# Who issues the six transfers that stack the second block's keys: SyncE's queue or ScalarE's

## The chip, the cores and the metric

The program runs on one core of a Trainium2 chip. The metric is the device time of one execution in microseconds (us). The core's engines run side by side, each through its own list of instructions, and wait for one another by semaphores: TensorE (PE in the profile; PEld is its weight load), VectorE (DVE), ScalarE (ACT), GpSimd (POOL) and SyncE (SP), which does nothing here but issue DMAs.

## The reference

32 images (12 x 224 x 224) are summed over patches of 16 x 16 and projected to 196 tokens of 192 channels; 77 text tokens are put behind them, so an image has T = 273 tokens. Two transformer blocks follow, each with 12 heads of 16 channels:

```
h = concat([tokens(x), txt])
h = h + quantised_attention_0(layernorm(h))
h = h + mixture_of_depth_block(layernorm(h))      # routed attention or mean mixing, then a GELU FFN
h = h + attention_1(layernorm(h))                 # softmax attention, what this change is about
h = h + experts(layernorm(h))                     # one shared and three routed SiLU experts, best two count
```

In `attention_1`, q and k are 12 x 273 x 16 each, and the scores q k^T are wanted nearly in float32 precision.

## The kernel before

The work on one image is cut into stages with short names. A turn, listed by hand in `TURN`, holds each stage once, for different images: a stage with offset 2 works on the image that a stage with offset 0 had two turns ago. Every engine goes through the stages of `TURN` in that order and does its own part of each, if it has one. There are 36 turns (32 images, and the turns in which the pipeline fills and drains); in steady state one turn finishes one image. TensorE's results go to four PSUM areas, A, B, M and N, with a pair of semaphores each: `full` (TensorE has written) and `taken` (it has been read, and the next stage may begin).

The change is at the start of a turn, in these stages:

- `n4f`: the normed tokens of the second block are transposed by TensorE and copied by ScalarE (L605).
- `qk1.0`, `qk1.1`: TensorE projects them to queries (area A) and keys (area B). ScalarE evicts each twice, as float32 (L654) and as bfloat16 (L658). VectorE makes two further bfloat16 pieces from the rest (L925 to L927), so that three pieces add up to nearly the float32 value. `parts_ready` counts 1 when the queries' pieces are there and 2 when the keys' are.
- The stack: a bfloat16 matmul over 96 rows gets the precise scores when the pieces are stacked, six blocks of 16 rows, in `q1s` and `k1s`. Each block is a transfer from `parts` (96 partitions) into 16 partitions of `q1s` or `k1s`; there are six for the queries and six for the keys, and all twelve count on `stack_in` (L457, issued by SyncE at `qk1.0` and `qk1.1`).
- `v2`: TensorE and VectorE.
- `n0f`: ScalarE copies the transposed tokens of another image (L599). `qk0.0`, `qk0.1`: TensorE and VectorE, then four small transfers each by SyncE (L450, `q0s` and `k0s`). `pool.0` between them: VectorE reduces a slice of an image, and SyncE issues the load of another one (L430).
- `n2f`: TensorE transposes, ScalarE copies with scale and bias (L584) and so frees area M. `ey.0`: TensorE (area A), `Silu` by ScalarE (L679). `v1`: TensorE, which needs the copy of `n2f` and area M (L1042), then VectorE (L828). `ez.0`: VectorE. `ey.1`: TensorE (area B).
- `mx.0`: the first of 36 matmuls (L1259) whose row maxima VectorE takes (L938). It waits for all twelve transfers of the stack. The other 35 are spread over the following third of the turn, between other stages.

`a0.0` (L1117), some way behind, is the first stage that waits for `q0s` and `k0s`. The queue of ScalarE holds only computation before the change.

Of the kernel before, what the change touches and what calls it, by code (L numbers as in the profile page):

```python
# [21 lines left out]
H, HD = 12, 16  # L22
# [18 lines left out]
Q_PARTS = (0, 0, 1, 0, 2, 1)  # L41
K_PARTS = (0, 1, 0, 2, 0, 1)
# [6 lines left out]


TURN = """
tok n4s n4n n4f cw n0s n1s n2n n0n qk1.0 qk1.1 v2 n0f qk0.0 pool.0 qk0.1 n2f ey.0 v1 ez.0 ey.1 mx.0 mx.1 mx.2 n1n gate
mx.3 ez.1 mx.4 pool.1 k1 mx.5 v0 a0.0 mx.6 mx.7 ey.2 cl.0 cl.1 ez.2 mx.8 r3 mx.9 mx.10 rta a0.1 cl.2 dy.0 cl.3 pk0
a0.2 mx.11 mx.12 mx.13 mx.14 mx.15 pk1 ey.3 ez.3 mx.16 r2 mx.17 gt mx.18 vs mx.19 pv.0 mx.20 og.0 mx.21 s1.0 mx.22
mx.23 s1.1 r1 mx.24 ey.4 ez.4 ey.5 mx.25 ez.5 t1.0 mx.26 mx.27 t1.1 mx.28 rtb mx.29 cl.4 mx.30 cl.5 a0.3 c1 mx.31
# [6 lines left out]
OFFSET = {"pool": -1}  # L62
OFFSET.update({x: 0 for x in "r2 tok n0s n0n n0f qk0 v0 vs a0 cl pv og pr0".split()})
OFFSET.update({x: 1 for x in ("r3 n1s n1n n2n n2f gate k1 v1 rta rtb pk0 gt pk1 s1 t1 c1 ct wo mg n3s n3n n3f f0 fd".split())})
OFFSET.update({x: 2 for x in "n4s n4n n4f r1 qk1 v2 mx mt a2 pw os ob pr1 n5s n5n n5f rtr".split()})
OFFSET.update({x: 3 for x in "cw ey ez dy".split()})
FIRST_TURN, LAST_TURN = -1, BATCH + 2

# [38 lines left out]
def early_fusion(nc, ins, out):  # L107
    pooled_dram = nc.dram_tensor("pooled_dram", (BATCH, CH, GRID, QUARTERS, GRID), F32).ap()
    ctx = ExitStack()
    with ctx:  # L110
# [37 lines left out]
        cw = sb("cw", [CH * QUARTERS, D])  # L148
# [66 lines left out]
        v1 = sb("v1", [KC, NC_, H, HD + 1])  # L215
# [195 lines left out]
        @block.sync  # L411
        def _(sp):
            sp.wait_ge(zeroed, 4)
            with nc.allow_non_contiguous_dma(reason="vectors onto partitions, once"):
                for dst, src in loads:
                    sp.dma_start(dst, src).then_inc(weights_in, 16)
            for k in range(NSLOT):
                sp.dma_start(img[:, k, :], img_dram[0, :, k, :]).then_inc(image_in[k], 16)

            def program(t):  # L420

                for stage in t.stages:
                    name, _, k = stage.partition(".")
                    k = int(k or 0)
                    n = t.image(stage)
                    if name == "pool":

                        sp.wait_ge(part_ready, n * XG + (k + 1))
                        if k < XG - NSLOT:
                            sp.dma_start(img[:, k % NSLOT, :], img_dram[n, :, k + NSLOT, :]).then_inc(image_in[k % NSLOT], 16)  # L430
                        elif n < BATCH - 1:
                            sp.dma_start(img[:, k % NSLOT, :], img_dram[n + 1, :, k - NSLOT, :])\
                                .then_inc(image_in[k % NSLOT], 16)
                        if k == XG - 1:

                            sp.dma_start(sums_dram[n], part[:, :, :]).then_inc(sums_out, 16)
                            sp.wait_ge(sums_out, n * 16 + 16)
                            if "tok" in t.stages:
                                t.await_taken("M", "tok")
                            for q in range(QUARTERS):  # L440
                                sp.dma_start(pooled[CH * q:CH * q + CH, :, :], pooled_dram[n, :, :, q, :]).then_inc(sums_in, 16)
                    elif name == "tok":

                        t.await_earlier_turns("M")
                        sp.dma_start(tokens0[TAIL:TC, 2, :], ins["txt"][n]).then_inc(text_in, 16)
                    elif name == "qk0":

                        sp.wait_ge((q0_ready, k0_ready)[k], t.done(stage))
                        for j in range(4):
                            sp.dma_start((q0s, k0s)[k][HP * j:HP * j + HD, :, :],  # L450
                                         qk0[HD * NG * (j % 2):HD * NG * (j % 2 + 1), k, j // 2, :])\
                                .then_inc((q0_in, k0_in)[k], 16)
                    elif name == "qk1":

                        sp.wait_ge(parts_ready, n * 2 + (k + 1))
                        for r, p_ in enumerate((Q_PARTS, K_PARTS)[k]):
                            sp.dma_start((q1s, k1s)[k][HD * r:HD * r + HD, :, :],  # L457
                                         parts[:, k, p_, :, :]).then_inc(stack_in, 16)
                    elif name == "mt":

                        sp.wait_ge(mrow_ready, t.done(stage))
                        for i in range(2):
                            sp.dma_start(q1s[SROWS + i:SROWS + i + 1, :, :], mrow[:, i, :]).then_inc(mrow_in, 16)
                    elif stage == "dy.3":
                        sp.wait_ge(out_ready, t.done(stage))
                        sp.dma_start(out[n].rearrange("(c p) d -> p c d", p=TC), outb[:, :, :]).then_inc(out_done, 16)

            go(sp, program)
            sp.wait_ge(out_done, 16 * BATCH + 1)

# [105 lines left out]
        def _(act):  # L576
# [11 lines left out]
            def program(t):  # L588
                for stage in t.stages:
# [60 lines left out]
                    elif name == "qk1":  # L650
# [6 lines left out]
                        for kc in range(NK):  # L657
                            last = a.activation(parts[:, k, 0, kc, :], area[x][0:KC, kc, 0:T], ACT.Identity,  # L658
                                                bias=b_qk1[:, k, kc:kc + 1])
                        last.then_inc(taken[x], 1)  # L660
                    elif name == "a2":
                        t.await_full(x, stage)

# [680 lines left out]
```

## Time and profile before

| | |
|---|---|
| three timed runs, us | 4804.51, 4835.94, 4847.9 (median 4835.94) |
| the profiled execution's own time, us | 4793.07 |
| its span, us | 4791.3 |
| TensorE busy | 4135.2 us, 86% of the span |
| VectorE busy | 2621.2 us, 55% |
| ScalarE busy | 1759.9 us, 37% |
| granted TensorE clock, mean | 0.855 |
| DMA through SyncE's queue | 153722 packets, 142.64 MB, 14.0% of 16 engines |

Times in the profile count from the start of its span. A row of a timeline merges neighbouring instructions of one kind: start, duration from the first start to the last end, what was done, how often, and in brackets how long the engine had been idle before it and who released it. The granted clock is a share of 2.4 GHz: 1.00 is 2.4 GHz and 0.50 is 1.2 GHz.

### The profile page before, as it was taken

The page shows a single profiled execution, that of the slowest core. Times are in us where ns is not written, and L with a number is a line of the kernel's source. Part 1 is how long each engine was busy: PE and PEld are TensorE (multiplying, and loading weights), DVE is VectorE, ACT ScalarE, POOL GpSimd, SP SyncE. Part 2 cuts the span into 40 slices and gives each one's busy share as a digit, 9 for nine tenths or more (in the row PEclk, how much of TensorE's full clock was granted, in tenths as well). Part 3 has the DMA queues.
Part 4 walks back from the last instruction along what each step waited for, and adds up shares of the span by engine and source line. Part 5 has one row for each costly group of instructions (what it writes and reads, how often), then busy time and mean ns, then how long its engine had stood idle before and what let it go on. Part 6 is the DMA issues. An engine that isn't in the chain of part 4 may idle for free.

```text
span 4791.3 us, 70127 instructions
## 1 busy us (share of the span) xinstructions
PE 4135.2 (86%) x27744; PEld 3228.1 (67%) x27744; DVE 2621.2 (55%) x7217; ACT 1759.9 (37%) x2774; POOL 402.3 (8%) x523
## 2 busy tenths in 40 slices
PE   2779888889888989888889888989889888989888
PEld 1556677676676767677676667767667776766666
DVE  2455555555655555555555655555655555565433
ACT  1234333334333334333334333344433333433332
POOL 2100000000000000000000000000000000000000
PEclk8678888888889888888888888888888888888888
DMA  4111111101111101111101111101111110111000
GB/s 113 31 27 34 32 26 36 33 21 34 32 26 36 33 21 34 32 26 36 33 21 34 32 29 34 36 17 34 36 32 26 36 33 21 34 26 16 13 13 4
DMA packets 154046, 147.13 MB, mean 31 GB/s; under 512 B 64359, under 2 KB 132026, under 8 KB 153722
## 3 DMA queue, kind: packets, MB, share of 16 engines
q1 hardware_dynamic: 153722, 142.64, 14.0%
q8 instruction: 223, 3.65, 0.3%
q14 instruction: 101, 0.83, 0.1%
HBM read 87.28 MB, written 7.91 MB: 20 GB/s over the span
## 4 chain that ended last, share of the span: by engine, by line
PE 62%; DVE 19%; SPq 5%; ACT 5%; DMA 4%; issue 3%; POOL 3%; POOLq 0%; DVEq 0%; ACTq 0%
PE area_a L1034 13%; PE area_n L1042 11%; PE area_b L1034 8%; PE area_m L1042 7%; SPq L457 5%; PE area_n L1259 4%; DMA k1s<-scratch 3%; PE area_n L1066 3%; DVE mx L938 3%; PE area_m L1209 2%; ACT pT_both L666 2%; PE area_a L1117 2%; PE area_b L1057 2%; DVE scratch L949 1%; PE area_m L1066 1%
## 5 line engine op out<-in xcount | busy, mean ns | idle before, releaser
L938 DVE TENSOR_REDUCE mx<-area_n 91x1 f32<-91x273 f32 x1152 | 472.1, 432 | 246.5 <-PE area_n L1259 236.1
L1042 PE MATMUL area_n<-w_dn,hid 128*91 128x192 f32 x2304 | 494.8, 380 | 46.5 <-DVE mrow L943 38.7
L1034 PE MATMUL area_a<-xT,w_gu 96*128 96x273 f32 x1536 | 446.4, 438 | 61.7 <-DVE y L898 38.2
L1042 PEld LDWEIGHTS area_n<-w_dn,hid 128*91 128x91 f32 x2304 | 426.4, 190 | 95.3 <-issue 60.3
L1259 PE MATMUL area_n<-k1s,q1s 96*91 96x273 bf16 x1152 | 350.1, 359 | 152.5 <-DVE mx L938 92.9
L1034 PE MATMUL area_b<-xT,w_gu 96*128 96x273 f32 x1536 | 430.3, 426 | 0.0
L1034 PEld LDWEIGHTS area_a<-xT,w_gu 96*128 96x128 f32 x1536 | 305.0, 208 | 154.2 <-DVE y L898 48.0
L1259 PEld LDWEIGHTS area_n<-k1s,q1s 96*91 96x91 bf16 x1152 | 142.3, 141 | 335.3 <-DVE mx L938 227.2
L1034 PEld LDWEIGHTS area_b<-xT,w_gu 96*128 96x128 f32 x1536 | 313.0, 208 | 73.1
L611 ACT ACTIVATE pa<-area_a,scal 91x820 bf16<-91x820 f32 x192 | 180.3, 939 | 302.3 <-PE area_a L1117 278.2
L949 DVE RECIPROCAL scratch<-area_n 128x273 f32<-128x273 f32 x96 | 179.1, 1866 | 157.1 <-PE area_n L1280 157.1
L1001 DVE SCALAR_TENSOR_TENSOR outb<-area_n,cwt,outb 91x192 f32<-91x192 f32 x288 | 102.1, 407 | 268.1 <-PE area_n L1042 268.1
L679 ACT ACTIVATE sg<-area_a 128x273 f32<-128x273 f32 x192 | 76.9, 401 | 437.7 <-PE area_a L1034 435.2
L666 ACT ACTIVATE pT_both<-area_a 91x820 f32<-91x820 f32 x192 | 162.8, 848 | 200.0 <-PE area_a L1057 197.3
L1034 PE MATMUL area_a<-xT,w_qk 96*96 96x273 f32 x512 | 196.0, 545 | 44.8 <-ACT xT L605 22.4
L679 ACT ACTIVATE sg<-area_b 128x273 f32<-128x273 f32 x192 | 76.6, 399 | 398.4 <-PE area_b L1034 398.1
L991 DVE TENSOR_TENSOR hid<-sg,area_a 128x273 f32<-128x273 f32 x192 | 83.5, 435 | 232.0 <-ACT sg L679 232.0
L755 DVE TENSOR_REDUCE part<-img 112x14 f32<-112x896 f32 x192 | 206.1, 1075 | 3.8 <-DMA img<-in_x 2.9
L679 ACT ACT_TABLE_LOAD x153 | 196.3, 1283 | 2.7
L1042 PE MATMUL area_m<-w,scratch 128*91 128x192 f32 x1152 | 194.7, 328 | 0.0
L1042 PEld LDWEIGHTS area_m<-w,scratch 128*91 128x91 f32 x1152 | 180.6, 159 | 6.6
L541 POOL TENSOR_TENSOR hb<-h,rows 91x576 f32<-91x576 f32 x64 | 89.5, 1398 | 1090.2 <-PE area_n L1259 1041.9
(242 smaller groups left out, 7595.4 us busy)
## 6 DMA issues: line engine op xcount, KB each, us to landing
img<-in_x SPq DMA_DIRECT2D x192, 392.0 KB, 3.4
q1s<-scratch SPq DMA_DIRECT2D x192, 102.4 KB, 3.4
k1s<-scratch SPq DMA_DIRECT2D x192, 102.4 KB, 4.4
out<-outb SPq DMA_DIRECT2D x32, 204.8 KB
q0s<-scratch SPq DMA_DIRECT2D x128, 25.6 KB, 3.6
k0s<-scratch SPq DMA_DIRECT2D x128, 25.6 KB, 2.8
pooled<-pooled_dram SPq DMA_DIRECT2D x128, 9.2 KB
tokens<-in_txt SPq DMA_DIRECT2D x32, 57.8 KB
```

The lines of the kernel that those rows point to most:

```text
L457: sp.dma_start((q1s, k1s)[k][HD * r:HD * r + HD, :, :], parts[:, k, p_, :, :]).then_inc(stack_in, 16)
L611: a.activation(pa[i][0:TC, :, :], area[x][0:TC, :, 0:W2C], ACT.Copy, bias=OFF, scale=col(C_P, TC)).then_inc(taken[x], 1)
L666: a.activation(pT[k % NPT][0:TC, :, :], area[x][0:TC, :, 0:W2C], ACT.Exp, scale=HD ** -0.5).then_inc(taken[x], 1)
L679: a.activation(sg[:, k % 2, :], area[x][:, 0, 0:T], ACT.Silu).then_inc(silu_ready, 1)
L755: v.tensor_reduce(part[:, k, :], img[:, k % NSLOT, :].rearrange("p (r j w) -> p j r w", r=Q_ROWS, j=GRID), AX.XY, ALU.add).then_inc(part_r ...
L938: v.tensor_reduce(mx[:, k:k + 1], N[0:TC, k % 2, 0:T], AX.X, ALU.max)\
L949: v.reciprocal(rec2[:, :], N[:, 1, 0:T]).then_inc(taken["N"], 1)
L1001: last = v.scalar_tensor_tensor(outb[:, c, :], by_token("N")[:, c, :], cwt[:, c, k - 1:k], outb[:, c, :], ALU.mult, ALU.add)
L1034: last = mm(area[x][0:rows_, j, 0:n], w(j, kc), rhs[:, kc, 0:n], start=(kc == 0), stop=(kc == NK - 1))
L1042: last = mm(by_token(x)[:, c, :], lhs(i, c), w_, start=(i == 0), stop=(i == len(w) - 1))
L1066: last = mm(area[x][HP * j:HP * j + HP, bank, to], v_(j)[:, c, :], p_(j)[:, at[0], at[1]], start=(i == 0), stop=(i == 3))
L1259: mm(N[0:TC, k % 2, 0:T], q1s[0:SROWS, hh, c * TC:(c + 1) * TC], k1s[0:SROWS, hh, :], start=True, stop=True).then_inc(full["N"], 1)
```

## The change

The six transfers of the keys are no longer issued by SyncE at `qk1.1`. A new stage `ks`, which only ScalarE has, stands behind `n0f` in the turn: ScalarE waits there until the keys' pieces are ready and issues the six transfers from its own queue. SyncE issues the queries' six at `qk1.0` as before and then goes on to the transfers of `qk0.0`. The transfers themselves, their number and size and the semaphore that they count on are unchanged.

```diff
-... v2 n0f qk0.0 pool.0 qk0.1 n2f ey.0 v1 ...
+... v2 n0f ks qk0.0 pool.0 qk0.1 n2f ey.0 v1 ...
@@ SyncE
-                    elif name == "qk1":
-
-                        sp.wait_ge(parts_ready, n * 2 + (k + 1))
-                        for r, p_ in enumerate((Q_PARTS, K_PARTS)[k]):
-                            sp.dma_start((q1s, k1s)[k][HD * r:HD * r + HD, :, :],
-                                         parts[:, k, p_, :, :]).then_inc(stack_in, 16)
+                    elif stage == "qk1.0":
+
+                        sp.wait_ge(parts_ready, n * 2 + 1)
+                        for r, p_ in enumerate(Q_PARTS):
+                            sp.dma_start(q1s[HD * r:HD * r + HD, :, :], parts[:, 0, p_, :, :]).then_inc(stack_in, 16)
@@ ScalarE, behind its part of qk1
+                    elif name == "ks":
+
+                        act.wait_ge(parts_ready, t.image(stage) * 2 + 2)
+                        for r, p_ in enumerate(K_PARTS):
+                            act.dma_start(k1s[HD * r:HD * r + HD, :, :], parts[:, 1, p_, :, :]).then_inc(stack_in, 16)
```

`ks` has offset 2, like `qk1`.

## Rows read from the trace of the kernel before

**Rows 1.** The page: shares of the chain by line, and the costliest groups (part 5)
```profile
PE area_a L1034 13%; PE area_n L1042 11%; PE area_b L1034 8%; PE area_m L1042 7%; SPq L457 5%; PE area_n L1259 4%; DMA k1s<-scratch 3%; PE area_n L1066 3%; DVE mx L938 3%; PE area_m L1209 2%; ACT pT_both L666 2%; PE area_a L1117 2%; PE area_b L1057 2%; DVE scratch L949 1%; PE area_m L1066 1%
...
L1259 PE MATMUL area_n<-k1s,q1s 96*91 96x273 bf16 x1152 | 350.1, 359 | 152.5 <-DVE mx L938 92.9
```

**Rows 2.** Line 457 alone: ns min/median/max, who waited for it, landing
```profile
L457 SPq DMA_DIRECT2D q1s<-scratch x192: 576/597/1992, 232.4 to 4652.1; - x192
...
  PE area_n L1259: 53.8, 32
...
DMA to landing us min/median/max: 2.9/3.9/5.3
```

**Rows 3.** The page, part 6: KB of one issue, median us to landing
```profile
img<-in_x SPq DMA_DIRECT2D x192, 392.0 KB, 3.4
...
k1s<-scratch SPq DMA_DIRECT2D x192, 102.4 KB, 4.4
```

**Rows 4.** Timeline of SyncE's queue at the starts of turns
```profile
367.54 3.83 SPq L457 DMA_DIRECT2D q1s<-scratch  x6
...
1229.69 3.86 SPq L457 DMA_DIRECT2D q1s<-scratch  x6
1233.59 3.79 SPq L457 DMA_DIRECT2D k1s<-scratch  x6
1237.42 2.50 SPq L450 DMA_DIRECT2D q0s<-scratch  x4
...
2523.69 5.13 SPq L457 DMA_DIRECT2D q1s<-scratch  x6
...
2670.49 5.02 SPq L457 DMA_DIRECT2D q1s<-scratch  x6
...
4077.03 3.85 SPq L457 DMA_DIRECT2D q1s<-scratch  x6
```

**Rows 5.** Timeline of TensorE up to `mx.0`, in three turns
```profile
1236.02 2.11 PE L1042 MATMUL area_m<-w_f,xT 96*91 96x192 f32 x12
1237.96 2.01 PE L1034 MATMUL area_b<-xT,w_gu 96*128 96x273 f32 x8
1241.87 0.69 PE L1259 MATMUL area_n<-k1s,q1s 96*91 96x273 bf16 x2 [1.90 <-DMA k1s<-scratch]
...
3389.06 0.43 PE L1259 MATMUL area_n<-k1s,q1s 96*91 96x273 bf16 x2 [0.30 <-DMA k1s<-scratch]
...
4520.53 0.69 PE L1259 MATMUL area_n<-k1s,q1s 96*91 96x273 bf16 x2 [5.66 <-DMA k1s<-scratch]
```

**Rows 6.** Timeline of ScalarE: the copies of `n0f` and `n2f`
```profile
1229.23 0.61 ACT L599 COPY xT<-area_m 96x546 f32<-96x546 f32 x1 [0.81 <-PE area_m L1025]
1234.34 1.04 ACT L584 ACTIVATE xT<-area_m,norm_gb 96x273 f32<-96x273 f32 x2 [4.49 <-PE area_m L1025]
...
3383.13 1.04 ACT L584 ACTIVATE xT<-area_m,norm_gb 96x273 f32<-96x273 f32 x2 [4.49 <-PE area_m L1025]
```

**Rows 7.** Timeline of VectorE: the last piece of the keys
```profile
1230.81 0.72 DVE L927 TENSOR_TENSOR scratch<-pT_both,scratch 96x546 bf16<-96x546 f32 x1
...
3378.56 0.72 DVE L927 TENSOR_TENSOR scratch<-pT_both,scratch 96x546 bf16<-96x546 f32 x1
```

**Rows 8.** Windows: length; busy us of PE, PEld, DVE, ACT, POOL; clock, DMA share, GB/s
```profile
1231.00:1232.00 1.00, 1.00 (x6) 0.72 (x5) 1.00 (x4) 0.00 (x0) 0.00 (x0) 1.00 0.70 180
1233.70:1239.70 6.00, 6.00 (x35) 5.20 (x33) 3.80 (x9) 2.73 (x4) 0.00 (x0) 1.00 1.11 128
...
1240.00:1249.00 9.00, 6.82 (x27) 5.03 (x28) 4.90 (x13) 1.94 (x3) 0.00 (x0) 0.62 0.37 69
...
3388.50:3390.00 1.50, 0.79 (x5) 0.25 (x4) 0.58 (x2) 1.18 (x2) 0.00 (x0) 1.00 0.92 243
...
1229.70:1373.10 143.40, 127.22 (x867) 99.73 (x867) 81.56 (x226) 55.45 (x88) 11.83 (x15) 0.87 0.15 31
3517.20:3656.90 139.70, 125.18 (x868) 97.87 (x867) 81.56 (x225) 55.25 (x88) 11.83 (x15) 0.88 0.16 31
```

More of the change, by code:

```diff
@@ L51 @@
 TURN = """
-tok n4s n4n n4f cw n0s n1s n2n n0n qk1.0 qk1.1 v2 n0f qk0.0 pool.0 qk0.1 n2f ey.0 v1 ez.0 ey.1 mx.0 mx.1 mx.2 n1n gate
+tok n4s n4n n4f cw n0s n1s n2n n0n qk1.0 qk1.1 v2 n0f ks qk0.0 pool.0 qk0.1 n2f ey.0 v1 ez.0 ey.1 mx.0 mx.1 mx.2 n1n gate
 mx.3 ez.1 mx.4 pool.1 k1 mx.5 v0 a0.0 mx.6 mx.7 ey.2 cl.0 cl.1 ez.2 mx.8 r3 mx.9 mx.10 rta a0.1 cl.2 dy.0 cl.3 pk0
@@ L64 @@
 OFFSET.update({x: 1 for x in ("r3 n1s n1n n2n n2f gate k1 v1 rta rtb pk0 gt pk1 s1 t1 c1 ct wo mg n3s n3n n3f f0 fd".split())})
-OFFSET.update({x: 2 for x in "n4s n4n n4f r1 qk1 v2 mx mt a2 pw os ob pr1 n5s n5n n5f rtr".split()})
+OFFSET.update({x: 2 for x in "n4s n4n n4f r1 qk1 ks v2 mx mt a2 pw os ob pr1 n5s n5n n5f rtr".split()})
 OFFSET.update({x: 3 for x in "cw ey ez dy".split()})
```

## The prediction

> **What bounds the kernel now.** I read the chain of waits by line first [rows 1]. Most of it is TensorE's matmuls, but two entries belong to one place: SyncE's issues of line 457 (5% of 4791.3 us) and the landing of `k1s` (3%). Together they are some 380 us, 12 us in each of the 32 turns: twelve issues one behind the other and one landing, at the start of every turn. That is how often the chain runs through the stack, not what the stack costs. TensorE has other work meanwhile, and what it really stands idle for the stack is 53.8 us over 32 waits [rows 2], 1.7 us a turn. That row is the ceiling of the direct gain.
>
> Then I read one turn engine by engine. The reader is to see that there are two kinds. In the turn that starts at 1229.69 TensorE ends `ey.1` at 1239.97 and `mx.0` starts at 1241.87, after an idle of 1.90; in the one at 3376.92 it ends at 3388.77 and waits 0.30 [rows 5]. From 367.54 to 2523.69 there are 15 turns of 143.7 us on average, from 2670.49 to 4077.03 ten of 140.7 [rows 4]. A turn of each kind side by side [rows 8]: TensorE is busy 127.2 and 125.2 us at a granted clock of 0.87 and 0.88. With the two levels 1.2 and 2.4 GHz that is 2 x 0.13 x 143.4 = 37 us and 2 x 0.12 x 139.7 = 34 us at the lower one. The 3.7 us between the turns are 1.6 of idle at `mx.0`, and the rest mostly matmuls at half clock: in the long turn the clock stands at 0.62 from 1240 to 1249, right behind the idle [rows 8]. So a shorter wait may give back more than itself.
>
> **Why the stack is late.** Two things could set it: the pitch of the issues, (3.86 + 3.79 + 0.04) / 12 = 0.64 us [rows 4], or the rate at which the transfers move. If only the pitch counted, the last issue would start at 1229.69 + 11 x 0.64 = 1236.7 and land 2.9 us later (the shortest landing, [rows 2]), at 1239.6. It landed at about 1241.8. By the rate: 102.4 KB each [rows 3] at the 128 GB/s of the window 1233.7 to 1239.7 [rows 8] is 0.82 us, so 1229.69 + 2.9 + 11 x 0.82 = 1241.6. The rate fits. In that window the DMA share is 1.11, so the engines look full. Yet two rows speak of another limit: early in the burst they move 180 GB/s, and when an image slice goes to 112 partitions 243 GB/s at a lower share of 0.92 [rows 8]. A stack transfer writes 16 partitions only. I take it that the narrow destination is slow, not the engines.
>
> **The change part by part.** Queries stay on SyncE: six issues from 1229.69, last one at 1232.9, landed 2.9 to 3.9 later [rows 2], by 1236.8.
>
> Keys go to ScalarE. Its copy of `n0f` ends at 1229.84 [rows 6]; VectorE's last piece of the keys is done at 1230.81 + 0.72 = 1231.53 [rows 7]. The new wait costs nothing by itself: ScalarE's next job, the `n2f` copy, comes at 1234.34 after 4.49 of idle [rows 6]. Six issues of 0.64 run from 1231.55 to 1235.39. ScalarE issues no DMA in this trace; the nearest rows are SyncE's, 0.58 to 1.99 us each, median 0.60 [rows 2]. I take the pitch of 0.64, since it is the same in all undisturbed turns, and keep 1.99 as the far end; below nothing is excluded, as an issue takes sequencer time. The `n2f` copy then starts 1.05 late and ends at 1236.44. Behind it wait TensorE's `v1`, the table load, and the `Silu` of `ey.0`. `v1` would have started at 1236.02 [rows 5], so it loses about 0.5; the `Silu` is 1 us later, and its reader on VectorE stands behind `v1`'s eviction anyway. `ey.1` ends at 1240.45.
>
> The last key issue starts at 1234.75. If keys and queries move side by side (other partitions, other limits) it lands 2.9 to 4.4 later (the shortest landing [rows 2], the median of the keys [rows 3]), by 1239.2. `mx.0` starts at 1240.5 instead of 1241.87: 1.4 us won. In the turn at 3376.92 the keys are ready at 3379.28 [rows 7], the six issues end at 3383.12, and the `n2f` copy was due at 3383.13 [rows 6]: no delay, and the whole wait of 0.3 goes; I take 0.5 as the mean of such turns, since the landing of the last transfer varies (2.9 to 5.3, [rows 2]).
>
> SyncE's queue is moved too: the four `q0s`, the image slice and the four `k0s` leave 3.8 us earlier. Nobody waits for them at this point; `a0.0` comes long after. What they cost is in the rivals.
>
> What is late next: TensorE itself, then the pace of the `mx` reductions, as now. The last two turns have little TensorE work, so that the stack alone sets `mx.0` (an idle of 5.66 at 4520.53, [rows 5]); there it comes as early as the last landing does, 1241.8 - 1239.2 = 2.6 us sooner in each.
>
> **The sum**, against the profiled execution (4793.07 us, span 4791.3). Direct only: 15 x 1.4 + 15 x 0.5 + 2 x 2.6 = 34, so 4759. With the clock: if each long turn becomes a short one, 15 x (143.7 - 140.7) = 45 in place of the 21, so 58 and 4735. The three timed runs have a median 43 us above the profiled one, which is what 12 to 14 more long turns make; I expect them to shrink likewise. Some will stay: a third of the turns at 3 us is 32. I forecast 4755, and for this case 4720 to 4785.
>
> **A rule against it.** The share of 1.11 says that the DMA engines are full [rows 8]. The Trainium skill, "DMA: Bandwidth & Descriptors", section "Issuing engines are not separate DMA queues", says that DMAs from any issuer interleave on the same 16 engines and that a second issuer only saves sequencer time; by it the stack would end when it does now and the sum would be no gain. "SBUF — State Buffer", section "Door 1: The DMA port swizzle", gives 16 partitions some 109 GB/s and other partitions other ports; by it two streams could add up, and the trace's 128 for the narrow and 243 for the wide destination agree. The same page reports only +6% from two DMAs on two halves. The first rule is the next rival.
>
> **Rivals.** (1) Slower: one stream after all. If the 128 GB/s is the limit of the engines, twelve transfers still need 12 x 0.82 us, and the last cannot land before 1241.6. Worse, the keys now share the engines with SyncE's next issues: `q0s` 102 KB from 1233.6 and an image slice of 392 KB [rows 3] right behind them, 3.83 before 1239.96, at 1236.1 [rows 4]. If about three key transfers (307 KB, 2.4 us) are left when the queries are through, at half the rate they need 4.8 us, and `mx.0` is up to 2.4 us later. The idle becomes 4.3 us; 32 x 2.4 = 77, with the clock up to 110, so 4910 to 4945. It decides if the joint rate stays under about 150 GB/s. For it: the share of 1.11. Against: 243 GB/s.
>
> (2) The same, but queues alternate by whole transfers, so that only two of the short `q0s` come between: `mx.0` within 0.4 us of now; 4836 to 4850.
>
> (3) Slower: ScalarE's issues are long. `mx.0` breaks even when `v1` is 1.9 us late, that is with issues ending at 1236.8, at (1236.8 - 1231.55) / 6 = 0.87 us each. At 1.2 each they end at 1238.75 and `mx.0` comes 2.0 later than now, 64 us in all: 4900. For it: the row's maximum of 1.99. Against: median 0.60, the same kind of issue.
>
> (4) The change does what it says, but the time won is waited out later in the turn: the reductions of `mx` or ScalarE's evictions set the pace between `mx.0` and `a0`. Turns keep their 143 us: 4815 to 4836. For it: TensorE already waits 92.9 us for these reductions before the `mx` matmuls [rows 1], 2.9 us a turn. Against: those waits are per reduction and move along with `mx.0`.
>
> **Chances.** Forecast 0.55, (4) 0.17, (2) 0.10, (1) 0.11, (3) 0.07. One per cent, 48 us, is about what a measurement of this kernel can tell from no change (its runs span 4804 to 4848). Faster by over 1% (below 4788): 0.54; within 1%: 0.29; slower: 0.17. Most of (1) and (3) is left out of the range, which is 4715 to 4865.
>
> **What the next profile would show.** ScalarE's queue with six issues of about 0.64 us between `n0f` and `n2f`; the `n2f` copy about 1 us later after Q is ready in the long turns; 150 GB/s or more in the stretch 3 to 6 us after the first query issue; waits for the stack at `mx.0` near nothing against 53.8 us; turns near 140 us. The forecast is wrong if the rate stays at 128, if the issues take over 0.87, or if the wait at `mx.0` goes and the turn keeps its length.

## The result and the profile after

| | median, us | runs |
|---|---|---|
| before | 4832.47 (4804.51 to 4847.9) | 15 |
| after | 4798.28 (4783.11 to 4819.35) | 15 |

The ratio is 0.9936, 95% interval 0.9916 to 0.9956: 31 us faster, where 81 were forecast (4755 against the median of 4836 then known). The profiled execution of the kernel with the change took 4798.28 us (span 4796.5, clock 0.856). The profiled execution of before, which the prediction is counted from, was one of its fast ones (4793.07). So the rows of after are set beside a second profile of before, taken for the experiments and called "before, again": 4843.92 us, span 4842.2, clock 0.851.

The page of after: the chain by line, TensorE's group for the `mx` matmuls, and the DMA issues (KB of one, median us to landing). They answer to [rows 1] and [rows 3]. The lines have moved: L1034 is L1038, L1042 is L1046, L1259 is L1263.

```profile
PE area_a L1038 14%; PE area_n L1046 11%; PE area_b L1038 10%; PE area_m L1046 7%; DMA k1s<-scratch 4%; PE area_n L1263 3%; PE area_n L1070 3%; DVE mx L942 3%; PE area_m L1213 2%; ACTq L664 2%; ACT pT_both L670 2%; PE area_a L1121 2%; PE area_b L1061 2%; DVE scratch L953 1%; PE area_m L1070 1%
...
L1263 PE MATMUL area_n<-k1s,q1s 96*91 96x273 bf16 x1152 | 345.7, 356 | 142.5 <-DVE mx L942 94.4
...
q1s<-scratch SPq DMA_DIRECT2D x192, 102.4 KB, 3.6
k1s<-scratch ACTq DMA_DIRECT2D x192, 102.4 KB, 6.0
...
q0s<-scratch SPq DMA_DIRECT2D x128, 25.6 KB, 6.3
k0s<-scratch SPq DMA_DIRECT2D x128, 25.6 KB, 5.2
```

SyncE's issues have gone from the chain (5% in [rows 1]), as wanted; ScalarE's stand in it with 2%. But the landing of `k1s` is in it with 4% in place of 3%, and a key transfer takes 6.0 us to land in place of 4.4. The line of the new issues alone shows the same (ns min/median/max; who waited; landing), beside [rows 2]:

```profile
L664 ACTq DMA_DIRECT2D k1s<-scratch x192: 568/620/1652, 235.3 to 4659.0; - x192
...
  PE area_n L1263: 43.4, 29
...
DMA to landing us min/median/max: 3.8/6.0/8.2
```

An issue costs ScalarE what it cost SyncE (620 ns against 597). TensorE still waits 43.4 us for the stack. Now one turn of after, which starts at 3531.96 when the queries' pieces are ready: timelines of SyncE, ScalarE and TensorE, to be read against [rows 4 to 6].

```profile
3531.99 4.04 SPq L457 DMA_DIRECT2D q1s<-scratch  x6
3536.16 2.48 SPq L450 DMA_DIRECT2D q0s<-scratch  x4
...
3533.87 3.84 ACTq L664 DMA_DIRECT2D k1s<-scratch  x6
3537.75 1.04 ACT L583 ACTIVATE xT<-area_m,norm_gb 96x273 f32<-96x273 f32 x2 [5.48 <-issue]
...
3538.85 2.19 PE L1046 MATMUL area_m<-w_f,xT 96*91 96x192 f32 x12 [0.25 <-ACT xT L583]
3540.87 2.01 PE L1038 MATMUL area_b<-xT,w_gu 96*128 96x273 f32 x8
3544.82 0.43 PE L1263 MATMUL area_n<-k1s,q1s 96*91 96x273 bf16 x2 [1.94 <-DMA k1s<-scratch]
```

And the windows of the same turn, which answer to [rows 8] (busy times; clock, DMA share, GB/s):

```profile
3533.50:3536.00 2.50, 2.50 (x12) 1.75 (x11) 2.43 (x7) 0.00 (x0) 0.00 (x0) 1.00 0.79 162
3536.00:3539.00 3.00, 2.75 (x17) 1.99 (x15) 2.57 (x5) 1.23 (x3) 0.00 (x0) 1.00 1.11 115
3539.00:3544.00 5.00, 3.88 (x20) 3.16 (x19) 1.23 (x4) 2.56 (x4) 0.00 (x0) 1.00 1.15 129
```

All twelve are issued by 3533.87 + 3.84 = 3537.71, 5.8 us after the queries are ready; before it was 1233.59 + 3.79 - 1229.69 = 7.7. Yet `mx.0` starts at 3544.82, 12.9 us after the queries are ready, against 1241.87 - 1229.69 = 12.2 before. From 3536 on, with keys and queries in flight together, the engines move 115 to 129 GB/s, what they moved with one queue (128, [rows 8]). The change moved the issues and not the transfers.

### The profile page after: what moved, and what is told of

It is laid out like the page before. It is cut to its first block, busy times and chain, and to the rows that moved or that the text cites. A ratio compares the mean times of both kernels' runs of the same rounds, so it can differ in the third digit from the quotient of the medians.

```text
span 4796.5 us, 70127 instructions
## 1 busy us (share of the span) xinstructions
PE 4139.1 (86%) x27744; PEld 3219.5 (67%) x27744; DVE 2620.1 (55%) x7217; ACT 1759.3 (37%) x2774; POOL 402.3 (8%) x523
## 4 chain that ended last, share of the span: by engine, by line
PE 65%; DVE 18%; ACT 5%; DMA 5%; issue 3%; ACTq 2%; POOL 2%; SPq 1%; DVEq 0%; POOLq 0%
PE area_a L1038 14%; PE area_n L1046 11%; PE area_b L1038 10%; PE area_m L1046 7%; DMA k1s<-scratch 4%; PE area_n L1263 3%; PE area_n L1070 3%; DVE mx L942 3%; PE area_m L1213 2%; ACTq L664 2%; ACT pT_both L670 2%; PE area_a L1121 2%; PE area_b L1061 2%; DVE scratch L953 1%; PE area_m L1070 1%
## 5 line engine op out<-in xcount | busy, mean ns | idle before, releaser
L1046 PE MATMUL area_n<-w_dn,hid 128*91 128x192 f32 x2304 | 489.8, 377 | 46.5 <-DVE mrow L947 38.7
L1038 PE MATMUL area_a<-xT,w_gu 96*128 96x273 f32 x1536 | 440.9, 433 | 62.0 <-DVE y L902 38.2
L1046 PEld LDWEIGHTS area_n<-w_dn,hid 128*91 128x91 f32 x2304 | 422.1, 188 | 94.0 <-issue 60.1
L1263 PE MATMUL area_n<-k1s,q1s 96*91 96x273 bf16 x1152 | 345.7, 356 | 142.5 <-DVE mx L942 94.4
L1038 PE MATMUL area_b<-xT,w_gu 96*128 96x273 f32 x1536 | 441.2, 435 | 0.0
L1038 PEld LDWEIGHTS area_a<-xT,w_gu 96*128 96x128 f32 x1536 | 301.8, 206 | 152.9 <-DVE y L902 48.0
L1038 PEld LDWEIGHTS area_b<-xT,w_gu 96*128 96x128 f32 x1536 | 318.4, 211 | 75.7
L1263 PEld LDWEIGHTS area_n<-k1s,q1s 96*91 96x91 bf16 x1152 | 142.1, 140 | 323.6 <-DVE mx L942 224.0
L1038 PE MATMUL area_a<-xT,w_qk 96*96 96x273 f32 x512 | 196.8, 547 | 44.8 <-ACT xT L604 22.4
L1046 PE MATMUL area_m<-w,scratch 128*91 128x192 f32 x1152 | 194.7, 328 | 0.0
L1046 PEld LDWEIGHTS area_m<-w,scratch 128*91 128x91 f32 x1152 | 180.6, 159 | 6.6
## 6 DMA issues: line engine op xcount, KB each, us to landing
q1s<-scratch SPq DMA_DIRECT2D x192, 102.4 KB, 3.6
k1s<-scratch ACTq DMA_DIRECT2D x192, 102.4 KB, 6.0
```

The lines of the kernel that those rows point to most:

```text
L1038: last = mm(area[x][0:rows_, j, 0:n], w(j, kc), rhs[:, kc, 0:n], start=(kc == 0), stop=(kc == NK - 1))
L1046: last = mm(by_token(x)[:, c, :], lhs(i, c), w_, start=(i == 0), stop=(i == len(w) - 1))
L1263: mm(N[0:TC, k % 2, 0:T], q1s[0:SROWS, hh, c * TC:(c + 1) * TC], k1s[0:SROWS, hh, :], start=True, stop=True).then_inc(full["N"], 1)
```

## The experiments

Ratios are to the kernel before on the same chip, with 95% intervals. To compare turns, each trace's 27 turns from the third to the 29th were measured from the rows: length of the turn (their numbers by kind, then the mean), start of `mx.0` after the queries' pieces are ready, and TensorE's wait there, both as means. The first row is the profile that the prediction was made from. A trace is one execution; the medians and ratios come from several.

| kernel | median us | ratio | turns of 140 or less / about 143 / over 145 us | mean | `mx.0` at | wait |
|---|---|---|---|---|---|---|
| before (profile of the prediction) | 4832.47 | 1 | 8 / 16 / 3 | 142.7 | +12.4 | 1.4 |
| before, again | 4829.16 | 1.0006 [0.9977, 1.0036] | 1 / 16 / 10 | 144.5 | +12.4 | 1.9 |
| after (first comparison) | 4798.28 | 0.9936 [0.9916, 0.9956] | 8 / 13 / 6 | 143.1 | +12.8 | 1.2 |
| after, again | 4790.87 | 0.9950 [0.9931, 0.9970] | 9 / 14 / 4 | 142.7 | +12.8 | 1.1 |
| SyncE holds back | 4802.49 | 0.9954 [0.9923, 0.9985] | 9 / 12 / 6 | 143.1 | +12.3 | 0.5 |
| ScalarE busy, 11 copies | 4768.31 | 0.9901 [0.9867, 0.9936] | 13 / 9 / 5 | 142.4 | +12.4 | 1.0 |
| ScalarE busy, 17 copies | 4804.21 | 0.9976 [0.9964, 0.9987] | 2 / 24 / 1 | 143.3 | +13.1 | 0 |
| keys issued later | 4954.53 | 1.0281 [1.0254, 1.0308] | 0 / 5 / 22 | 148.2 | +15.0 | 4.2 |
| early start | 4703.40 | 0.9763 [0.9730, 0.9796] | 27 / 0 / 0 | 139.9 | +10.4 | 0 |
| rows six apart | 4688.81 | 0.9725 [0.9696, 0.9754] | 27 / 0 / 0 | 139.8 | +10.6 | 0 |
| the change, rows six apart | 4702.21 | 0.9745 [0.9720, 0.9771] | 24 / 1 / 2 | 139.8 | +11.7 | 0 |
| early start, rows six apart | 4688.35 | 0.9735 [0.9718, 0.9752] | 27 / 0 / 0 | 139.9 | +10.7 | 0 |
| before, four matmuls in the wait | 4705.46 | 0.9763 [0.9739, 0.9787] | 27 / 0 / 0 | 140.0 | +13.5 | 0 |
| before, seven | 4803.41 | 0.9961 [0.9945, 0.9977] | 0 / 26 / 1 | 143.5 | +14.2 | 0 |
| the change, four | 4765.30 | 0.9893 [0.9854, 0.9932] | 16 / 8 / 3 | 141.7 | +13.7 | 0 |

**Before and after, again.** Nothing is edited.

> The kernel before, unchanged, timed against itself. Both theories: ratio 1.000 within 0.003. Its profile tells what the profiled execution of before (4793, 40 us under the median) does not: I expect 20 or more of the 31 turns at 143.3 us or longer, where that one had 17, and about 1.7 to 2.1 us of idle before mx.0 in those.

> The kernel with the change, unaltered, in another call: its time and its trace a second time, to see how far the turn lengths of one execution are the same in the next. Theory: the ratio to the kernel before is again 0.992 to 0.996 (4795 to 4815), the stack lands 12.3 to 13.7 us after the queries are ready, and turns of about 140, 143 and 146 us are mixed. Rival (the gain is an accident of the runs taken so far): a ratio of 0.998 to 1.003.

The kernel before against itself gives 1.0006, and the second comparison of the change agrees with the first. The gain of 0.5 to 0.6% is real. Turns come in lengths of about 140, 143 and 147 us. Against the trace of before, again, the change has more of the short kind (8 and 9 against 1). But the first trace of before, an execution of 4793 us, has 8 as well: the mixture differs that much between executions of one kernel, so that one trace of each does not carry a gain of this size. The medians do.

**What limits the transfers.** Bursts of twelve transfers of 102.4 KB (KB of 1024 bytes) run once, ahead of the kernel's own work; each burst waits for the one before. The first starts while images are still being loaded.

```diff
+for i, burst in enumerate((stack, wide, same, hbm)):
+    for dst, s_ in burst:
+        sp.dma_start(dst, s_).then_inc(bench[i], 16)
+    sp.wait_ge(bench[i], 16 * 12)
+...                                                 # then stack and wide again, SyncE six and ScalarE six
```

> Once, ahead of the work, SyncE moves six bursts of twelve transfers, waiting for each burst: (1) the stack's form, 96 partitions to 16, (2) the same bytes and packets 96 to 96 partitions, (3) 16 partitions to 16 in long rows, (4) from memory to 16 partitions, (5) the stack's form with six of the twelve issued by ScalarE, (6) form 2 with six issued by ScalarE. Theory 'narrow destination': 1, 3 and 4 at 110 to 130 GB/s, 2 and 6 at 200 or more (bounded by the issue pitch of 0.64 us, 160 GB/s, where one queue issues), 5 faster than 1. Theory 'engines': 1, 2, 5 and 6 all at about 128 GB/s. The rest of the kernel is that of before; its one time is about 60 us longer.

`stack` goes from 96 into 16 neighbouring partitions, `wide` from 96 into 96, `same` from 16 into 16 neighbours in long rows, `hbm` from memory into 16. Windows of five of the bursts, in order: `stack` by one queue; `wide` by one; `same` by one; `stack` by two queues; `wide` by two.

```profile
44.00:50.00 6.00, 0.00 (x0) 0.00 (x0) 5.86 (x8) 0.00 (x0) 0.00 (x0) 1.00 1.11 152
56.00:60.00 4.00, 0.00 (x0) 0.00 (x0) 0.00 (x0) 0.00 (x0) 0.00 (x0) 1.00 0.59 168
66.00:69.00 3.00, 0.00 (x0) 0.00 (x0) 0.00 (x0) 0.00 (x0) 0.00 (x0) 1.00 0.86 166
...
84.00:90.00 6.00, 0.00 (x0) 0.00 (x0) 0.00 (x0) 0.00 (x0) 0.00 (x0) 1.00 1.12 113
96.00:99.00 3.00, 0.00 (x0) 0.00 (x0) 0.00 (x0) 1.28 (x1) 0.00 (x0) 1.00 0.96 274
```

A second queue lifts the wide form from 168 to 274 GB/s: there the pitch of the issues was the limit (102.4 KB every 0.63 us is 166). It does not lift the stack's form, which goes from 152 to 113. In both bursts of that form the share stands above 1.1 although the engines move 41 to 55% of the 274. So the limit is neither the issue nor what the sixteen engines can move. It is not the number of partitions written either: `same` was expected at 110 to 130 and takes 166, the pitch again, into the same 16 neighbours at a share of 0.86. (`hbm`, partly in transfers of 34.1 KB, moves 121 at the same share.) The packets of `same` have 6552 bytes, those of `stack` and `wide` 1092. What is slow is the stack's form: short packets from 96 partitions into neighbouring rows. `same` differs in both, packet and source, and which of the two makes it faster is not shown. Here both queues wrote the same groups of 16 partitions. The second set has the ScalarE queue three groups away from SyncE's, as in the change, and adds a destination of 16 rows that are six apart.

> Bursts of twelve transfers in the stack's form ahead of the work, each alone on an idle core: (1) one queue, neighbouring rows; (2) one queue, rows 6 apart; (3) two queues, neighbouring rows, in the order of the change (keys three groups of rows away from the queries); (4) two queues, rows 6 apart. In the first set of bursts one queue with neighbouring rows made 152 GB/s, two queues on the same groups of rows 114, 96 rows from two queues 274. If different groups of 16 rows can be written at the same time, 3 is faster than 1; if the narrow form is slow as such, 3 is at 115 to 150. 2 at the pitch of the issues, 160 GB/s with a low DMA share; 4 at 250 or more.

```profile
49.00:55.00 6.00, 0.00 (x0) 0.00 (x0) 3.31 (x5) 0.00 (x0) 0.00 (x0) 1.00 1.03 138
61.00:66.00 5.00, 0.00 (x0) 0.00 (x0) 0.00 (x0) 0.00 (x0) 0.00 (x0) 1.00 0.59 166
71.00:77.00 6.00, 0.00 (x0) 0.00 (x0) 0.00 (x0) 0.00 (x0) 0.00 (x0) 1.00 1.12 127
82.00:86.00 4.00, 0.00 (x0) 0.00 (x0) 0.00 (x0) 1.28 (x1) 0.00 (x0) 1.00 1.09 232
```

Neighbouring rows, one queue: 138 GB/s; two queues, groups apart: 127. The 138 holds the first transfers, before they pile up; from 51 to 56 it is 126 at a share of 1.12. From the first issue to the last landing the burst takes 12.0 us by one queue and 11.9 by two, though two have issued it all in 4.1 us and one needs 7.7. So two queues are neither slower nor faster. Rows six apart: 166 by one queue, at a share of 0.59, and 232 by two; 9.2 and 7.9 us. The packets have the same 1092 bytes in both forms, and a single one takes 121 ns in the median into neighbouring rows and 49 into rows six apart. Other groups of partitions do not add up when each transfer's own 16 rows are neighbours; the same bytes spread over the partitions do.

**Rows six apart.** The same twelve transfers on SyncE; each piece goes to rows r, r + 6, r + 12, ... of the stack, for queries and keys alike, so the sums over 96 rows are the same.

```diff
-sp.dma_start((q1s, k1s)[k][HD * r:HD * r + HD, :, :],
+sp.dma_start((q1s, k1s)[k][r:SROWS:6, :, :],
```

> The kernel before, but each of the twelve transfers writes 16 rows that lie 6 apart (r, r+6, ..., r+90) instead of 16 neighbours; queries and keys alike, so the scores are the same. Everything stays on SyncE. Theory 'narrow destination': the rate is no longer the bound, the pitch of the issues is: the last lands 11 x 0.64 + 2.9 = about 10.0 us after the queries are ready instead of 12.2, mx.0 comes at 10.4 in a long turn, and the ratio is 0.980 to 0.990. Theory 'engines, or the source': no change, 1.000 within 0.003.

> The change, with the rows 6 apart. If the destination was what the prediction missed, this is the change as it was forecast: the last transfer lands by 9.5 us after the queries are ready, mx.0 waits only for TensorE (at 10.9), and the ratio is 0.980 to 0.988 (forecast 4755 of 4836 was 0.983). If it is worth no more than the same rows with SyncE alone, the second queue has nothing to give once the destination is wide. If neither: the stack still lands at 12.3 or later, 0.990 to 0.996.

The timeline of the turn that starts at 1200.84, without the change:

```profile
1209.18 2.01 PE L1034 MATMUL area_b<-xT,w_gu 96*128 96x273 f32 x8
1211.02 0.40 PE L1259 MATMUL area_n<-k1s,q1s 96*91 96x273 bf16 x2
```

No wait stands at `mx.0`: it follows `ey.1` directly, 10.2 us after the queries are ready. The stack has landed at +9.3, and every turn is of the short kind: 2.75% faster, one slice in the code, and more than the expected 1 to 2%. With the change on top the stack lands at +8.9 in the mean of the 27 turns, as early as the prediction had it (by +9.5). It gains nothing over SyncE alone and is 13 us slower by the medians (4702.21; the intervals overlap): ScalarE's issues push `v1` from +6.8 to +7.8, and `mx.0` follows at +11.7 in place of +10.6.

**Early start.** All on SyncE; the six transfers of the pieces that ScalarE writes itself start before VectorE's pieces are there.

```diff
-sp.wait_ge(parts_ready, n * 2 + (k + 1))
-(six transfers)
+t.await_taken("AB"[k], stage)
+stack(k, True)              # the pieces that ScalarE wrote: three transfers
+if k:
+    for k_ in range(2):
+        sp.wait_ge(parts_ready, n * 2 + (k_ + 1))
+        stack(k_, False)    # the others: three each
```

> All on SyncE, but the three transfers of the queries' bfloat16 piece start when ScalarE has written it, 3.1 us before the queries' other pieces are ready, and the three of the keys' as well; the other six follow. If the stream of transfers is the bound (0.82 us each), the last lands at 8.9 us after the queries are ready instead of 12.2, and mx.0 waits for TensorE alone: 34 us less by the waits alone (ratio 0.993), 60 to 80 less if the clock follows (0.984 to 0.988). If the pitch of the issues were the bound, the landing would come forward too, so this run does not tell these two apart; if the turn is set by something behind mx.0 the wait goes and the ratio stays above 0.998.

> The kernel before with both of the edits that brought the stack forward: the six transfers of the pieces that ScalarE writes start before VectorE's pieces are there, and each transfer writes 16 rows that are six apart in place of 16 neighbours. Theory (TensorE's own work sets mx.0 in either of the two alone, so the stack has nothing left to give but in the last two turns, 2 x 3 to 5 us): 4680 to 4695, and no wait for the stack in the list. Rival (the stack's landing still sets mx.0 in some turns of each): 4650 to 4675.

```profile
1206.53 1.87 SPq L458 DMA_DIRECT2D k1s<-scratch  x3
1208.45 1.87 SPq L458 DMA_DIRECT2D q1s<-scratch  x3
1210.36 1.88 SPq L458 DMA_DIRECT2D k1s<-scratch  x3
...
1217.74 0.40 PE L1267 MATMUL area_n<-k1s,q1s 96*91 96x273 bf16 x2
```

Started earlier at the same rate, the stack lands at about +9.9, and the time falls by 2.4%, where 0.7 or with the clock up to 1.6% was expected. Both together give no more than rows six apart alone (4688.35 and 4688.81).

**SyncE holds back.** The change, but SyncE issues `q0s`, the image slice and `k0s` only when the stack has landed.

```diff
 sp.wait_ge((q0_ready, k0_ready)[k], t.done(stage))
+if stage == "qk0.0" and "qk1.0" in t.stages:
+    sp.wait_ge(stack_in, t.image("qk1.0") * STACK_DMAS + STACK_DMAS)
```

> The change, but SyncE holds back q0s, the image slice and k0s until all twelve stack transfers have landed. Both queues then carry stack transfers only. If q0s between the keys' transfers cost what the change lost against the run with ScalarE merely busy (0.9936 against 0.990), the last lands at 12.2 instead of 12.8 and the ratio is about 0.990. If two queues are slow by themselves, it still lands at 12.5 or later and the ratio stays at 0.993 or above.

The mean landing comes 0.7 us sooner (+12.1 against +12.8), so these transfers do take rate from the keys. The time stays where it was (4802.49): of the two expectations the landing met the first and the ratio the second. So the later landing is not what the change lacks against the 0.990 below.

**Keys issued later.** The change with `ks` behind `n2f`.

```diff
-... v2 n0f ks qk0.0 pool.0 qk0.1 n2f ey.0 ...
+... v2 n0f qk0.0 pool.0 qk0.1 n2f ks ey.0 ...
```

> The change with the new stage one place later: ScalarE issues the keys' six transfers behind the n2f copy, not ahead of it. Theory (what the change gains is a by-product of the late n2f copy and the late v1 behind it; the stack itself lands later and only costs): the n2f copy is at its old place, some 4.6 us after the queries are ready, the key issues run from about +5.7 to +9.5 and the stack lands at +12.8 to +13.5, TensorE's wait at mx.0 grows to about 2.5 us a turn, and the time is no shorter than that of the kernel before: 4825 to 4860. Rival (the second queue itself gives the gain, since SyncE goes on earlier to q0s, the image slice and k0s): these leave as early as in the change, so the gain of 30 us stays, 4790 to 4810.

```profile
L1263 PE MATMUL area_n<-k1s,q1s 96*91 96x273 bf16 x1152 | 365.0, 374 | 236.9 <-DMA k1s<-scratch 139.2
```

The wait for the stack, 43.4 us in the change, is 139.2, and the kernel is 2.8% slower. The size was missed by some 100 us. I had not counted the clock: against before, again, TensorE is busy 52 us more for the same work (4216.8 against 4165.3 us) and idle 59 more. The run tells against the second queue as the source of the gain, but not cleanly: it moves the stack's landing too, by 2.2 us.

**ScalarE busy.** The kernel before, all transfers on SyncE. Where the change has ScalarE issue, it makes 11, or 17, small copies that nobody reads, each waiting for the last.

```diff
+elif name == "ks":
+    act.wait_ge(parts_ready, t.image(stage) * 2 + 2)
+    for _ in range(BUSY):
+        a.copy(idle_out[:, :], ones[:, :]).then_inc(idle_done, 1)
+        idles[0] += 1
+        act.wait_ge(idle_done, idles[0])
```

> All twelve stack transfers stay on SyncE; ScalarE only does eleven small copies where it would issue, so that the n2f copy comes about 1 us late in the long turns. Theory 'split idle' (the stack lands when the transfers are through, whoever issues; the change gains because v1 comes later, which breaks the idle before mx.0 in two and spares TensorE a stretch at 1.2 GHz): the same gain as the change, ratio 0.991 to 0.996. Rival 'SyncE is free earlier' (the gain comes from q0s, the image slice and k0s leaving 3.8 us sooner): 1.000, or slower, since ScalarE only loses time.

> As act_busy (all twelve transfers on SyncE, ScalarE makes small copies where the change has it issue DMAs), but 17 copies in place of 11, so that the n2f copy starts about 8.5 us after the queries are ready and no longer 5.5. Adds work that nobody uses. Theory (a late v1 splits TensorE's idle time in front of mx.0 and the turn falls to a shorter length): v1 is some 3 us later than in act_busy, ey.1 ends at about +13.5 and the wait for the stack, landed at +12.5, is gone, but mx.0 is later than before, by about 1.3 us a turn: 4780 to 4830, no better than act_busy's 4768. Rival (any later n2f copy is good, the more the better): 4720 to 4760.

With 11 copies the `n2f` copy starts about 0.9 us late, as in the change, and nothing else is touched. The stack lands and `mx.0` starts when they did, and the kernel is 1.0% faster, more than the change itself gives. With 17 copies the wait at `mx.0` is gone and `mx.0` is 0.7 later, and most of the gain is lost. In single turns the clock behind the wait differs. Windows of one turn each, the 24 us that begin 12 us after the queries are ready. Before, again:

```profile
1244.90:1268.90 24.00, 21.37 (x129) 17.11 (x129) 17.00 (x52) 7.82 (x14) 1.40 (x1) 0.79 0.12 35
1268.90:1376.20 107.30, 95.80 (x689) 74.73 (x688) 56.77 (x158) 42.90 (x70) 10.40 (x14) 0.87 0.08 19
```

ScalarE busy, 11 copies, a turn of 140.2 us and one of 143.0:

```profile
958.30:982.30 24.00, 21.01 (x146) 17.23 (x147) 19.20 (x58) 9.11 (x14) 1.39 (x1) 0.93 0.13 37
982.30:1086.50 104.20, 93.52 (x664) 72.75 (x663) 54.45 (x150) 41.32 (x67) 10.42 (x14) 0.85 0.08 20
...
1098.50:1122.50 24.00, 20.77 (x143) 16.47 (x144) 19.02 (x58) 10.31 (x15) 1.40 (x1) 0.93 0.13 38
1122.50:1229.50 107.00, 96.32 (x675) 74.76 (x673) 54.72 (x152) 42.04 (x68) 10.43 (x14) 0.84 0.07 19
```

In the first pair TensorE works equally long in the 24 us (21.4 and 21.0) but gets 146 matmuls done in place of 129, at a clock of 0.93 in place of 0.79. At the levels 1.2 and 2.4 GHz, 0.79 is 2 x 0.21 x 24 = 10 us at the lower one, 0.93 is 3. Before, again, the first stretch at half speed stands right behind TensorE's wait for the stack. The rest of the turn goes the other way, 0.85 against 0.87, and the turn of 143.0 us shows that the window does not decide the length: it has 0.93 too. The means over the 27 turns say how much is left over the whole turn:

| kernel | clock, the 24 us | clock, behind them | clock, whole turn | TensorE busy, us | idle, us |
|---|---|---|---|---|---|
| before (profile of the prediction) | 0.84 | 0.86 | 0.866 | 127.3 | 15.4 |
| before, again | 0.75 | 0.87 | 0.861 | 128.4 | 16.1 |
| after | 0.88 | 0.85 | 0.867 | 127.5 | 15.6 |
| ScalarE busy, 11 copies | 0.87 | 0.85 | 0.867 | 127.3 | 15.0 |
| ScalarE busy, 17 copies | 0.86 | 0.84 | 0.858 | 128.2 | 15.1 |
| early start | 0.87 | 0.87 | 0.878 | 125.5 | 14.4 |
| before, four matmuls in the wait | 1.00 | 0.85 | 0.890 | 125.8 | 14.2 |

Most of what the later `n2f` copy wins in the 24 us is given back behind them. With 17 copies the window stands as with 11, and the gain is gone: there TensorE's busy time is what it was before, again. And the first trace of before stands close to after in every column but the first. So that the delay makes the kernel faster is shown by the runs; that it does so by the clock behind `mx.0` is only suggested by these traces.

**Matmuls in the wait.** This tests whether idle time ahead of `mx.0` costs clock: before `mx.0` waits, TensorE multiplies weights that lie ready into the bank that `mx.0` overwrites. Nobody reads the results, no transfer and no other engine is touched.

```diff
+t.begin_bank("N", stage, "mx")        # was behind the wait
 if k == 0:
+    for _ in range(FILL):       # 4 or 7
+        mm(N[0:TC, 0, 0:T], w_qk1[:, 0, 0:TC], w_qk1[:, 0, 0:T], start=True, stop=True)
     pe.wait_ge(stack_in, n * STACK_DMAS + STACK_DMAS)
```

> The kernel before, with seven matmuls on TensorE ahead of its wait for the stack at mx.0 (float32, 96 x 91 by 273 columns of the weights of the second block's queries, 0.25 us each, into the bank of area N that mx.0 overwrites): they fill the idle time of about 1.9 us and nobody uses them. The stack lands when it did. Theory A (what the wait costs is above all the clock: TensorE standing idle right ahead of mx.0 brings it to half speed just behind): mx.0 starts no earlier, at +12.2, but the half-clock stretch from +12 on is gone, the long turns shrink although nothing was brought forward, and the time falls to 4750 to 4800. Theory B (the wait costs its own length, the clock goes its own way): the same as before, 4825 to 4845, or more, as in the turns in which TensorE waits only 0.5 the fill is 1.3 too long (up to 4850).

> As b_fill with four of the matmuls in place of seven, 1.0 us: it leaves some 0.9 us of idle time ahead of mx.0 in the long turns, and is 0.5 too long in the short ones. Theory A: part of the gain, 4770 to 4815; by how much it differs from b_fill tells how long an idle time the clock still notices. Theory B: 4825 to 4845.

> The kernel with the change and the same four matmuls as in b_fill4. Theory A (the change gained only because ScalarE's late copy moves TensorE's idle time from the wait for the stack to the place ahead of v1, which spares the clock; its stack lands 0.3 to 0.6 us later): with the idle time filled in both, the change has nothing left to give and is slower than b_fill4 by the later landing, 30 x 0.3 to 0.6, 9 to 18 us. Rival (the second queue gives something of its own): it keeps its lead of 30 us over b_fill4.

I had the size of the fill wrong: a float32 product of 273 columns is two instructions of 0.25 us, so four are 2.0 us and seven 3.5. Four fill the wait of 1.9 us just so. Timeline and window of one turn (it starts at 1215.32):

```profile
1225.15 2.01 PE L1035 MATMUL area_b<-xT,w_gu 96*128 96x273 f32 x8
1227.00 2.00 PE L1258 MATMUL area_n<-w_qk 96*91 96x273 f32 x8
1228.84 0.40 PE L1262 MATMUL area_n<-k1s,q1s 96*91 96x273 bf16 x2
...
1227.30:1251.30 24.00, 21.22 (x154) 17.00 (x153) 19.11 (x58) 10.24 (x15) 1.39 (x1) 1.00 0.12 36
```

Useless work makes the kernel 2.4% faster, as much as the early start of the transfers does. The stack lands at +12.4 as before, and `mx.0` starts at +13.5, 1.1 us later than before; still all 27 turns are of the short kind. The clock in the 24 us is 1.00, and TensorE ends 154 instructions there in place of 129. Over the whole turn TensorE is busy 2.6 us less than before, again, although 2.0 us of useless work are in it. That is theory A of the expectation, and stronger than it stood there (4770 to 4815). Seven are 1.5 us more a turn and make it 3.5 us longer; their time of 4803.41 is just above the expected range.

The change with the same four is 60 us slower than without the change, where 9 to 18 were expected. In its one trace the first turns, the third to the 15th, are all 140.0 or less. Then ScalarE's six issues take longer, in two turns running. Queue and engine in the second:

```profile
2466.08 5.04 ACTq L665 DMA_DIRECT2D k1s<-scratch  x6
2471.16 1.04 ACT L584 ACTIVATE xT<-area_m,norm_gb 96x273 f32<-96x273 f32 x2 [5.76 <-issue]
```

5.04 us in place of 3.84, and the copy behind them is as much later. This turn lasts 146.1 us, and those after it are mixed. In the kernel without the change SyncE's issues vary likewise, and no computation stands behind them. Not all is told by that: a later turn of 146.3 us has its six issues in 3.85.

## Why the prediction was wrong, step by step

**Right in an undisturbed turn: the sizes on the issuing side.** In the turn shown, ScalarE pays 3.84 us for six issues (0.64 each, as taken), the `n2f` copy is 1.1 us late (1.05 said), and `v1` comes at 6.89 - 6.33 = 0.56 late (0.5 said). SyncE's later transfers leave 3.5 us earlier (3.8 said). In the mean of the 27 turns it is more: the six take 4.2 us, over 4.2 in 11 turns and 5.35 at most (0.89 each), and `v1` comes at +7.7 against +7.1 and +6.5 in the two traces of before, so 0.6 to 1.2 late. Rival (3), long issues, is out for the median (620 ns).

**Right, with a limit: what set the landing.** "The rate fits" holds. "The narrow destination is slow, not the engines" holds for the stack's form: 113 to 152 GB/s into 16 neighbouring partitions, up to 274 into 96. It is too wide as it stands, since 16 neighbours take 166 in long packets from 16 partitions.

**The step that failed: "If keys and queries move side by side (other partitions, other limits)".** They don't. Two queues into groups of 16 rows that are apart move 127 GB/s, one moves 126 to 138, and a burst of twelve takes 11.9 and 12.0 us. In the kernel it was 115 to 129 GB/s where the prediction named 150 or more, and 128 as the sign of being wrong. I took the low rate for a limit of each destination group, from which it seemed to follow that two groups have twice the rate. The trace of before could not tell this: it shows one stream at a time. The stack was therefore to land by +9.5 and lands at +12.8 on average. The Trainium skill, "DMA: Bandwidth & Descriptors", section "Issuing engines are not separate DMA queues", says that DMAs of any issuer interleave on the same 16 engines and that a second issuer saves only the time of the issue. The trace agrees: issue time was saved and was not the bound. The Trainium skill, "SBUF — State Buffer", section "Door 1: The DMA port swizzle", gives 109 GB/s for 16 partitions; here streams of transfers into one group of 16 after the other made 113 to 166. My reading of it, that other partitions add up, did not hold for two streams of this kind. The change with rows six apart repairs this step alone: the stack then lands at +8.9.

**A second term, too small.** There the forecast of `mx.0`, 1240.45 - 1229.69 = +10.8 when only TensorE is waited for, is missed as well: it comes at +11.7. ScalarE's delay cost `v1` 1.0 us and not 0.5. Without the second queue the same rows give +10.6.

**Rivals.** The mechanism of (2) and (1), one stream after all, is what happened. In the change it cost 0.5 us of landing a turn on average, near (2)'s 0.4. But neither time came: both said slower or the same, and the kernel is 31 us faster, since no rival had the effect of ScalarE's delay. With the keys issued behind `n2f`, `mx.0` is 2.6 us later, near (1)'s 2.4, and the kernel takes 4954.53 (4910 to 4945 was (1)'s range). Rival (4), that turns keep their length, is out: without the wait they are 4.6 us shorter on average (139.9 against 144.5).

**The sum.** Its direct terms, 34 us, rest on the failed step and are nil: `mx.0` is later, not earlier. The wait fell from 71.3 us (before, again) or 53.8 to 43.4 because TensorE comes later, not because the stack is sooner. Of the 81 us forecast only 38 came from the sum (4793 to 4755). The other 43 were the distance of the profiled execution from the median, to be won by the long turns shrinking "likewise"; they rest on the same step. The rivals were counted from the median, so the two are not on one base. Its second idea, that "a shorter wait may give back more than itself", was right and too small. The wait of 53.8 us [rows 2] was called "the ceiling of the direct gain", and 45 us allowed with the clock. Taking the wait away gives 2.4 to 2.75%, 114 to 133 us of some 4820. The early start shows how it adds up, against before, again. The waits for the stack fall from 71.3 to 11.7 us, 60 less. TensorE's busy time falls from 4165.3 to 4083.3 us for the same work, 82 less. Together 142, and the spans differ by 141. The clock gives nearly the same, as an estimate: time at the lower level falls from 2 x 0.149 x 4842 = 1443 to 2 x 0.135 x 4702 = 1270 us, 173 less, which is 87 us of matmuls. So the clock was worth more than the wait.

**Where the 31 us come from.** Not from the transfers: the stack lands later. ScalarE's issues delay the `n2f` copy, and with it `v1`, and ScalarE's delay alone gives 1.0%. With the wait filled, the change only costs. This much is shown. That the delay helps because part of TensorE's idle time moves ahead of `v1` and shortens the half-speed stretch behind `mx.0` is argued: the stretch is shorter, but most of it comes back later in the turn, and with 17 copies the gain is lost with the same clock there. Why the change gives 0.5 to 0.6% and not 1.0 is open too; the scatter of ScalarE's issues is a candidate, and the later landing is not, since with SyncE holding back it was gone and the time was the same. Why the clock falls for longer behind one arrangement of idle time than behind another, and why turns come in steps of some 3.4 us, so that the next 1.5 us of fill cost 3.5, stays open.

## What to carry to other kernels

Before a second queue is added, find what the transfers wait for: the pitch of the issues or the rate. A DMA share above 1 does not mean that the engines give all they can; compare the GB/s with those of a wide transfer in the same trace. If short packets into neighbouring rows are slow, spread the rows over the partitions; that was one slice here and gave 2.75%, while the second queue gave 0.6% by accident.

Cost a wait of TensorE by what its busy time changes over whole turns, and not by the wait's own length; the clock in the window right behind it tells only a part, and so does one turn. A quick test whether it matters is to fill it with matmuls that nobody needs. And a DMA that a computing engine issues puts the scatter of the issues into the computation.

## What was not expected of the hardware

- Four useless products (2.0 us a turn) in front of a wait make the kernel 116 us faster: clock 1.00 in place of 0.75 in the 24 us that start 12 us after the queries are ready, in the mean of 27 turns.
- Sixteen rows six apart take 166 GB/s at a DMA share of 0.59 where sixteen neighbours take 138 at 1.03; with two queues 232 against 127.
- Two queues into the same 16 neighbouring rows move 113 GB/s, less than one (152 in the same run, 126 to 138 in the other); into groups apart they move what one does (11.9 and 12.0 us for twelve transfers).
- Sixteen neighbouring rows are not slow as such: long packets (6552 bytes, from 16 partitions) go into them at 166 GB/s, short ones (1092 bytes, from 96) at 113 to 152.
